# A graph network's attention layers: GpSimd gathers all source rows, with a pause for landing every 16, and TensorE's one-hot gathers go

## The chip, the cores and the metric

The kernel runs on one core of one Trainium2 chip. The metric is device time in microseconds of one execution; the kernel before takes 4386.61 us, the median of 3 runs (4384.65 to 4387.99).

## The reference

Four graph layers on 3125 nodes with 128 features and 100,000 edges, sorted by destination. Each is followed by a residual add and a layer norm. The first is a two-step GCN; the other three are attention layers (4, 8 and 4 heads), and the change is in these. Cut to what matters:

```python
x = (h @ W).reshape(n, H, C)                 # a row of 128 features per node
score = leaky_relu(a_src[src] + a_dst[dst])  # H numbers per edge
m = segment_max(score, dst);  p = exp(score - m[dst])
den = segment_sum(p, dst)
out = segment_sum(x[src] * (p / den[dst])[:, :, None], dst)
```

So every edge needs the row x[src] of its source node and that node's H source scores. The output has 3125 x 128 float32 values.

## The kernel before, in words

**Steps, blocks, groups.** 128 edges lie on the 128 partitions and make one step. A step never mixes two tiles of 128 destination nodes, so the 782 edge tiles become 806 real steps (REAL_STEPS). Eight steps are a block (U), 64 a group (GROUP); there are 101 blocks and 13 groups. The last group begins at step 760, so group 11 has 56 steps and group 12 has 46.

**A layer** is a `node_stage` (norms, the product with the weights, the table of rows written to HBM, per-node scores scattered to HBM by GpSimd, line 2016) and then `attend`. In `attend` a ring of 128 slots in SBUF (two groups) holds the gathered rows `m.ring`. For a group the order is:

- the rows arrive in the ring: GpSimd issues an indirect DMA per step, line 1400, each fetching 128 rows of 132 or 136 floats by the indices in `m.src`. It may reuse a slot when TensorE has finished the product of the step that held it (`product`);
- ScalarE copies the rows' score columns (line 1458), TensorE transposes them (line 1514), VectorE computes scores and running maxima (`score`, first line 1608), ScalarE takes exponentials;
- for each block: VectorE multiplies the rows by their coefficients (`message`, line 1685) and makes a one-hot of destinations (`onehot`, line 1691), TensorE multiplies the two (line 1554, two passes per step in the trace), VectorE adds the product to the node sums (`add_up`, line 1722), step by step at places that it loads into registers;
- VectorE prepares the destination scores of the next group (`spread`).

**TensorE's gathers.** Six of each group's 64 steps (AIDED) aren't gathered by DMA. The table is kept in SBUF as three bfloat16 parts that add up to float32 (`m.thirds`, made in `node_stage`, lines 1900, 1906, 1959, 1985). SyncE loads the six steps' source numbers broadcast to all partitions (line 1416). For 25 node tiles times two passes of three steps (50 units) ScalarE (lines 1439 and 1442) or VectorE (line 1387) makes a one-hot of sources, and TensorE multiplies it with the three parts (line 1497, three matmuls per unit) into three PSUM banks. VectorE adds the three parts and puts the rows into the ring (`take_aided`, lines 1701 to 1703). The units are laid by hand between the group's other work: CHAIN_HOTS, PART_HOTS and GAP_HOTS say how many go where, PART_DVE which of them VectorE makes. Group 0's units run at the start of the layer, those of group g+1 during group g.

**Queues.** GpSimd's queue in `attend` holds nothing but the waits for ring slots and the gathers. SyncE's queue holds, per group, the masks, the source numbers and the destination scores; the last wait in group 0 until the scatters of `node_stage` have landed (`m.scattered`), which is line 1424's first load.

Of the kernel before, what the change touches and what calls it, by code (L numbers as in the profile page):

```python
# [49 lines left out]
AIDED = 6  # L50
HOTS = 12
CHAIN_HOTS = (6, 2, 4)
PART_HOTS = (3, 3, 3, 4, 4, 4, 4, 4)
PART_DVE = (1, 1, 1, 1, 1, 1, 1, 1)
GAP_HOTS = (6, 3)
TAKEN_IN = (4,)
MIDDLE = NODE_TILES * P // 2
AHEAD_HOTS = sum(CHAIN_HOTS)
PASSES = AIDED // PER_BANK
UNITS = PASSES * NODE_TILES  # L60
WIDE_HOT = PER_BANK * P
# [17 lines left out]
assert AHEAD_HOTS + sum(PART_HOTS) + sum(GAP_HOTS) == UNITS and len(PART_HOTS) * U == GROUP and AIDED % PER_BANK == 0  # L79
assert CHAIN_HOTS[0] <= HOTS and AHEAD_HOTS <= HOTS and len(TAKEN_IN) == PASSES - 1  # L80
assert all(AHEAD_HOTS + sum(PART_HOTS[0:b]) == (n + 1) * NODE_TILES for n, b in enumerate(TAKEN_IN))
# [69 lines left out]
def allocate(nc, ctx, m):  # L151
# [20 lines left out]
    m.src_rows = m.arena[:, late:late + LANES // 2].bitcast(F16).rearrange("p (g e) -> p g e", e=P)  # L172
    assert late + LANES // 2 <= ARENA
# [27 lines left out]
    m.tile_low = sb("node_number_middle", [P, NODE_TILES])  # L201
    m.low_tile = sb("middle_node_number", [P, NODE_TILES])
# [19 lines left out]
    words = NODE_TILES * W // 2  # L222
    m.all_thirds = m.arena[:, at:at + 3 * words].bitcast(BF16).rearrange("p (t j f) -> p t j f", t=3, f=W)
    m.thirds = [m.all_thirds[:, i] for i in range(3)]
    at += 3 * words
    words = AIDED * P // 2
    m.aid_rows = [m.arena[:, at + h * words:at + (h + 1) * words].bitcast(F16) for h in range(2)]
    at += 2 * words
    words = WIDE_HOT // 2
    m.aid_far = [m.arena[:, at + h * words:at + (h + 1) * words].bitcast(F16) for h in range(2)]  # L230
    at += 2 * words
    m.aid_hot = [m.arena[:, at + h * words:at + (h + 1) * words].bitcast(BF16) for h in range(HOTS)]
    at += HOTS * words
# [20 lines left out]
    m.d_src_rows = dram("source_rows", [LANES, P], F16)  # L254
# [577 lines left out]
def load_counts_and_sum(nc, m, a):  # L832
# [28 lines left out]
    def mask(name):  # L861
# [3 lines left out]
         weights_in, rel_known, turned, rows_known, open_known, masks_known, stored) = phase(  # L865
        nc, "chunk_loaded_0", "chunk_loaded_1", "chunk_product", "unit_summed", "last_loaded", "dve_step", "begin_known", "begin_spread",
        "tiles_known", "j_turned", "j_out", "j_stored", "edges_gathered", "weights_gathered", "rel_known", "edges_turned",
        "source_rows_known", "open_known", "masks_known", "masks_stored")
# [4 lines left out]
    with ph, nc.Block(no_gpsimd_drain=True) as block:  # L873
# [15 lines left out]
        def _(sp):  # L889
# [14 lines left out]
            sp.wait_ge(rows_known, 1)  # L904
            sp.dma_start(m.d_src_rows.rearrange("(g p) e -> p g e", p=P), m.src_rows).then_inc(stored, 16)
# [3 lines left out]
            sp.wait_ge(stored, 48)  # L909
# [55 lines left out]
        def _(dve):  # L965
# [19 lines left out]
            def steps_known():  # L985
                chain(dve.tensor_tensor(j_of, step, t_of, ALU.subtract))
                chain(dve.tensor_copy(m.step_tile[:], t_of))
                chain(dve.tensor_scalar(m.step_base[:], j_of, float(P), None, ALU.mult))
                chain(dve.tensor_scalar(j_cap, j_of, float(NODE_TILES - 1), float(F + 8), ALU.min, ALU.mult))
                dve.engine_nop().then_inc(tiles_known, 1)  # L990
                chain(dve.memset(m.row_keep[:], 0.0))
                chain(dve.memset(m.row_back[:], NEG))
                chain(dve.tensor_scalar(m.tile_low[:], m.node_no[:], -float(MIDDLE), None, ALU.add))
                chain(dve.tensor_scalar(m.low_tile[:], m.tile_low[:], -1.0, None, ALU.mult))

            def edges_known():
# [5 lines left out]
                dve.tensor_scalar(m.src_rows, src, -float(MIDDLE), None, ALU.add).then_inc(rows_known, 1)  # L1002
# [288 lines left out]
def attend(nc, m, H, a, weighted, self_loops):  # L1291
# [12 lines left out]
    aid_banks = m.psum[:, 5 * 512:8 * 512].rearrange("p (k c) -> p k c", c=512)  # L1304
# [5 lines left out]
             "group_scored", "cleared", "aid_rows_in_0", "aid_rows_in_1", "far_known", "aid_hot_act", "aid_hot_dve", "hot_used", "aid_taken",  # L1310
             "table_back", "dve_step")
# [3 lines left out]
         group_scored, cleared, aid_rows_in0, aid_rows_in1, far_known, hot_act, hot_dve, hot_used, aid_taken, table_back, dve_step) = phase(nc, *names)  # L1315
    masks_in, spread_in = (masks_in0, masks_in1), (spread_in0, spread_in1)
    aid_rows_in = (aid_rows_in0, aid_rows_in1)
# [10 lines left out]
    def place(s):  # L1328
        g = sum(s >= lo_of(k) for k in range(1, GROUPS))
        return s - lo_of(g)  # L1330

# [17 lines left out]
    by_dve = set()  # L1349
    part_of = []  # L1350
    for n, own in zip(PART_HOTS, PART_DVE):
        lo = part_of[-1][-1] + 1 if part_of else AHEAD_HOTS
        part_of.append(range(lo, lo + n))
        by_dve.update(part_of[-1][n - own:])
    in_gap = range(UNITS - sum(GAP_HOTS), UNITS)

    def parts_of(g, b):
        blocks = blocks_of(g)
        return range(b - blocks[0], len(part_of) if b == blocks[-1] else b - blocks[0] + 1)

    def made_by_dve(g, u):
        return u % 2 == 1 if g == 0 else u in by_dve

    def made(g, u):
        return sum(made_by_dve(k, v) == made_by_dve(g, u) for k in range(g + 1) for v in range(UNITS if k < g else u + 1))

    def tails_of(g):
        return sum(1 + (lo_of(k) % SLOTS + size_of(k) > SLOTS) for k in range(g + 1))

    def hot_of(g, u):  # L1370
        return m.aid_hot[(g * UNITS + u) % HOTS]

    def rows_of(g, u):
        return m.aid_rows[g % 2][:, u // NODE_TILES * WIDE_HOT:(u // NODE_TILES + 1) * WIDE_HOT]

    def wait_for_hot(eng, g, u):
        n = g * UNITS + u
        if n >= HOTS:
            eng.wait_ge(hot_used, n - HOTS + 1)
        if u == 0 or g == 0 or u in by_dve:  # L1380
            eng.wait_ge(aid_rows_in[g % 2], 16 * (g // 2 + 1))

    def hot_on_dve(dve, g, u):
        wait_for_hot(dve, g, u)
        hi = u % NODE_TILES
        odd = lambda view: view.rearrange("p (a e) -> p a e", a=3)
        dve.tensor_scalar(odd(hot_of(g, u)), odd(rows_of(g, u)), m.tile_low[:, hi:hi + 1], None, ALU.is_equal).then_inc(hot_dve, 1)  # L1387
# [4 lines left out]
    with ph, nc.Block() as block:  # L1392

        @block.gpsimd
        def _(pool):
            for b in range(BLOCKS):
                if b * U >= SLOTS:
                    pool.wait_ge(product, min((b + 1) * U, REAL_STEPS) - SLOTS)
                for s in gathered(b):
# [4 lines left out]
        def _(sp):  # L1404
            for g in range(GROUPS):
# [26 lines left out]
        def _(act):  # L1432
            far = [0]

            def hot_on_act(g, u):
                wait_for_hot(act, g, u)
                hi = u % NODE_TILES
                away = m.aid_far[far[0] % 2]
                act.activation(away, rows_of(g, u), ACT.Abs, bias=m.low_tile[:, hi:hi + 1]).then_inc(far_known, 1)  # L1439
# [878 lines left out]
```

## Time and profile before

| | |
|---|---|
| three runs | 4384.65, 4386.61, 4387.99 us |
| the profiled execution | span 5825.1 us; no other time of it is on record |
| instructions in the trace | 61632 |
| busy: PE, DVE, ACT, POOL | 3173.4, 3165.7, 2409.4, 2312.0 us |
| mean granted TensorE clock | 0.753 |

The profiled execution's span is 1438.5 us longer than the median of the runs. Times in the rows are microseconds from the start of the span, unless marked ns. PE is TensorE's matmul, PEld its weight load, DVE is VectorE, ACT ScalarE, POOL GpSimd, SP SyncE; L1400 is line 1400 of the kernel. A row's last part, after the bar or in brackets, is idle time of the engine before the instruction and what ended it, as far as the profile can tell.

### The profile page before, as it was taken

To read this page: it belongs to the slowest core of one execution; us is meant where nothing else is said; L and a number is where in the kernel's file an instruction comes from. 1 tells how busy PE (TensorE), PEld (TensorE's weight loads), DVE (VectorE), ACT (ScalarE), POOL (GpSimd) and SP (SyncE) were. 2 spreads that over 40 slices of the span, in tenths; PEclk is the share of its full clock that TensorE was granted. 3 is DMA by queue.
4 is the path that set the end of the run, shared out by engine and by line. 5 is a ranking of instruction groups with operands and counts; after the bars stand their busy time and mean duration, and the time that the engine had idled before them with its cause. 6 is when DMAs were issued, how large, how long until landed. Compare 5 with 4: busy or idle time off the path is not lost. (4 is left out here: it accounts for less than half of the span.)

```text
span 5825.1 us, 61632 instructions
## 1 busy us (share of the span) xinstructions
PE 3173.4 (54%) x16208; PEld 1958.6 (34%) x16208; DVE 3165.7 (54%) x10115; ACT 2409.4 (41%) x5229; POOL 2312.0 (40%) x2409
## 2 busy tenths in 40 slices
PE   2888787623555555562155554555523555564563
PEld 1333343312333333342033333333311333343342
DVE  5999853513454554576064464555822455454466
ACT  0766630023444444443143443444433444444453
POOL 3000002074555455415545545544064545545422
PEclk7999998856777677786577777777756777777786
DMA  2111124221212222111112212211021212212110
GB/s 75 60 60 60 60 85 168 99 62 36 48 46 48 47 47 50 42 28 37 42 45 48 52 44 48 50 46 44 4 55 37 47 47 47 50 45 47 45 25 23
DMA packets 127624, 298.46 MB, mean 51 GB/s; under 512 B 45412, under 2 KB 74972, under 8 KB 123712
## 3 DMA queue, kind: packets, MB, share of 16 engines
q0 software_dynamic: 74976, 155.58, 11.6%
q1 hardware_dynamic: 52320, 139.24, 7.1%
q8 instruction: 116, 1.90, 0.1%
q14 instruction: 212, 1.74, 0.1%
HBM read 241.28 MB, written 53.38 MB: 51 GB/s over the span
## 5 line engine op out<-in xcount | busy, mean ns | idle before, releaser
L1400 POOL DMA_INDIRECT work<-table,lane_src x2184 | 2072.7, 949 | 1897.4 <-PE psum L1554 967.3
L1439 ACT ACTIVATE work<-work,middle_node_number 128x384 f16<-128x384 f16 x1587 | 958.0, 604 | 1997.8 <-DMA work<-table,lane_src 950.8
L1497 PE MATMUL psum<-work 128*128 128x396 bf16 (+1 forms) x5850 | 1360.1, 380 | 699.7 <-issue 464.9
L1554 PE MATMUL psum<-work 128*128 128x136 f32 x4836 | 827.7, 339 | 1004.9 <-DVE node_sums L1722 890.6
L1722 DVE TENSOR_TENSOR node_sums<-node_sums,psum 128x136 f32 x2418 | 561.3, 294 | 1455.8 <-remote 892.2
L1554 PEld LDWEIGHTS psum<-work 128*128 128x128 f32 x4836 | 778.8, 242 | 1085.0 <-issue 969.9
L1497 PEld LDWEIGHTS psum<-work 128*128 128x128 bf16 x5850 | 626.3, 109 | 1290.0 <-issue 758.1
L1442 ACT ACTIVATE work<-work 128x384 bf16<-128x384 f16 x1587 | 829.4, 523 | 50.4
L715 PE MATMUL psum<-work 128*128 128x448 f16 x2100 | 460.9, 358 | 47.4 <-issue 37.5
L744 DVE TENSOR_SCALAR work<-work 128x400 f16<-128x400 f16 x1568 | 468.3, 320 | 0.0
L772 PE MATMUL psum<-work 128*128 128x400 f16 x1568 | 342.1, 342 | 111.8 <-DVE work L744 90.9
L1685 DVE TENSOR_TENSOR work<-work,psum 128x1024 f32<-128x1024 f32 (+1 forms) x303 | 367.3, 1213 | 7.3 <-ACT work L1477 4.4
L1691 DVE TENSOR_TENSOR work<-psum,lane_dst_rel 128x1024 f32<-128x1024 f32 (+1 forms) x303 | 365.1, 1216 | 1.3
L880 POOL DMA_INDIRECT work<-in_dst,step_edge_tile x7 | 6.7, 951 | 829.3 <-DVEq L990 827.4
L743 DVE TENSOR_SCALAR work<-work 128x128 f16<-128x128 f16 x1176 | 295.0, 251 | 10.0 <-PE psum L772 5.9
L715 PEld LDWEIGHTS psum<-work 128*128 128x128 bf16 x2100 | 207.7, 99 | 232.8 <-issue 59.4
L810 ACT CAST work<-psum 128x400 f16<-128x400 f32 x392 | 192.9, 492 | 188.0 <-PE psum L772 184.1
L1701 DVE COPY work<-psum 128x396 f32<-128x396 f32 (+1 forms) x78 | 44.6, 571 | 368.9 <-DMA work<-table,lane_src 209.6
L709 DVE TENSOR_TENSOR node_sums<-node_sums,psum 128x16 f32 x784 | 132.5, 169 | 204.6 <-issue 183.4
L772 PEld LDWEIGHTS psum<-work 128*128 128x128 f16 x1568 | 127.0, 99 | 332.8 <-DVE work L744 193.1
L1387 DVE TENSOR_SCALAR work<-work,node_number_middle 128x384 bf16<-128x384 f16 x363 | 112.9, 319 | 223.6 <-DMA work<-table,lane_src 81.0
L2016 POOL DMA_INDIRECT spread<-node_spread,node_pos_first x75 | 72.8, 971 | 327.8 <-DVEq L1893 263.4
(360 smaller groups left out, 2539.9 us busy)
## 6 DMA issues: line engine op xcount, KB each, us to landing
counts<-work SPq DMA_DIRECT2D x14, 2800.0 KB, 8.1
work<-counts SPq DMA_DIRECT2D x14, 2800.0 KB
work<-table,lane_src POOLq DMA_INDIRECT x2184
work<-spread SPq DMA_DIRECT2D x78, 256.0 KB
work<-masks SPq DMA_DIRECT2D x78, 128.0 KB
work<-source_rows SPq DMA_DIRECT2D x39, 192.0 KB
spread<-node_sums SPq DMA_DIRECT2D x4, 896.0 KB
table<-work SPq DMA_DIRECT2D x10, 330.0 KB
```

Source lines behind the costliest of these rows:

```text
L715: t = pe.matmul(sum_bank(m, q), m.parts[part][:, hi, :], m.counts[q][:, :, hi * CW:(hi + 1) * CW], start=(hi == 0 and part == 0), stop=(hi ...
L743: dve.tensor_scalar(m.hot_lo[:, d, b, :], m.iota_cols[:, 0:P], m.low[:, b, bass.ds(n, 1)], None, ALU.is_equal)
L744: t = dve.tensor_scalar(m.hot_key[:, d, b, :], m.iota_cols[:], m.key[:, b, bass.ds(n, 1)], None, ALU.is_equal)
L772: t = pe.matmul(unit_bank(k), m.hot_lo[:, d, b, :], m.hot_key[:, d, b, :], start=(b == 0), stop=(b == CB - 1))
L1400: pool.indirect_dma_start(m.ring[:, s % SLOTS, 0:F + H], None, m.d_table[H], bass.IndirectOffsetOnAxis(ap=m.src[:, s:s + 1], axis=0)).then ...
L1439: act.activation(away, rows_of(g, u), ACT.Abs, bias=m.low_tile[:, hi:hi + 1]).then_inc(far_known, 1)
L1442: act.activation(hot_of(g, u), away, ACT.Relu, bias=1.0, scale=-1.0).then_inc(hot_act, 1)
L1497: mm = pe.matmul(aid_banks[:, k, 0:3 * (F + H)], hot_of(g, u)[:, k * P:(k + 1) * P], m.all_thirds[:, :, hi, 0:F + H], start=(hi == 0), sto ...
L1554: pe.matmul(sum_slot(s), m.onehot[b % 2][:, s % U, :], m.ring[:, s % SLOTS, :], start=True, stop=True).then_inc(product, 1)
L1685: dve.tensor_tensor(rows, rows, over(coef.unsqueeze(3), [P, n, H, C]), ALU.mult).then_inc(messages, 1)
L1691: dve.tensor_tensor(m.onehot[b % 2][:, 0:n, :], over(counted.unsqueeze(1), [P, n, P]), over(m.drel[:, b * U:b * U + n].unsqueeze(2), [P, n ...
L1722: dve.tensor_tensor(to, to, sum_slot(s), ALU.add).then_inc(summed, 1)
```

## The change

GpSimd gathers every step (`steps_of(b)` in place of `gathered(b)`). Before the gathers of each even block but the first it waits until those of the two blocks before have landed (`rows_in` at `landed(k)`). All of TensorE's gathers go: the one-hots on ScalarE and VectorE, the matmuls, the takes, the broadcast loads, the thirds of the table in `node_stage` and the source rows stored in the set-up. In `node_stage` the product of block b waits for the copies to the table (`tables`) where it waited for the thirds. The products of a block of steps use two alternating sets of three PSUM banks, where there was one set, so that a product waits for the sums of two blocks before.

```diff
-AIDED = 6
-HOTS = 12
-CHAIN_HOTS = (6, 2, 4)
-PART_HOTS = (3, 3, 3, 4, 4, 4, 4, 4)
...
-    def gathered(b):
-        return [s for s in steps_of(b) if place(s) >= AIDED]
-
     def landed(b):
-        return 16 * sum(len(gathered(k)) for k in range(b, -1, -(SLOTS // U)))
+        return 16 * sum(len(steps_of(k)) for k in range(b, -1, -(SLOTS // U)))
...
     def sum_slot(s):
-        at = (2 + s % U // PER_BANK) * 512 + s % U % PER_BANK * W
+        at = (2 + s // U % 2 * BLOCK_BANKS + s % U // PER_BANK) * 512 + s % U % PER_BANK * W
         return m.psum[:, at:at + W]
...
                 if b * U >= SLOTS:
                     pool.wait_ge(product, min((b + 1) * U, REAL_STEPS) - SLOTS)
-                for s in gathered(b):
+                if b % 2 == 0 and b:
+                    for k in (b - 2, b - 1):
+                        pool.wait_ge(rows_in[k % (SLOTS // U)], landed(k))
+                for s in steps_of(b):
                     pool.indirect_dma_start(m.ring[:, s % SLOTS, 0:F + H], None, m.d_table[H],
...
-                if g >= 2:
-                    sp.wait_ge(hot_used, (g - 1) * UNITS)
-                sp.dma_start(m.aid_rows[g % 2], m.d_src_rows[own.start:own.start + AIDED, :].rearrange("(a s) e -> a (s e)", a=1)
-                             .to_broadcast([P, AIDED * P])).then_inc(aid_rows_in[g % 2], 16)
...
-                    if b == blocks_of(g)[0]:
-                        act.wait_ge(aid_taken, (g + 1) * PASSES)
-                    if gathered(b):
-                        act.wait_ge(rows_in[b % (SLOTS // U)], landed(b))
+                    act.wait_ge(rows_in[b % (SLOTS // U)], landed(b))
...
-                if g + 1 < GROUPS:
-                    for u in range(AHEAD_HOTS, UNITS):
-                        if u not in by_dve:
-                            hot_on_act(g + 1, u)
...
-            aid(0, range(UNITS))
             turn_spread(0)
...
-                        if s % U % PER_BANK == 0 and s >= U:
-                            pe.wait_ge(summed, bank_end(s - U))
+                        if s % U % PER_BANK == 0 and s >= 2 * U:
+                            pe.wait_ge(summed, bank_end(s - 2 * U))
...
-                    for n in parts_of(g, b):
-                        aid(g + 1, part_of[n])
...
-            for u in range(UNITS):
-                if u % 2:
-                    hot_on_dve(dve, 0, u)
-                if u % NODE_TILES == NODE_TILES - 1:
-                    take_aided(0, u // NODE_TILES)
...
-                    if g + 1 < GROUPS and n in TAKEN_IN:
-                        take_aided(g + 1, TAKEN_IN.index(n))
...
-                    dve.tensor_tensor(product, product, high[:, j, :], ALU.subtract).then_inc(rest_known, 1)
...
-                    dve.tensor_tensor(low[:, j, :], out_part(b, n)[:, :, 0:F + H], middle[:, j, :], ALU.subtract).then_inc(thirds_known, 1)
...
                 if b >= 2:
-                    pe.wait_ge(thirds_known, len(parts) * (b - 1))
+                    pe.wait_ge(tables, per_block * (b - 1))
...
-                    act.copy(middle[:, j, :], out_part(b, n)[:, :, 0:F + H]).then_inc(middle_taken, 1)
...
-                    act.copy(high[:, c * BLK + lo:c * BLK + hi, :], out_part(c, n)[:, :, 0:F + H]).then_inc(high_taken, 1)
```

## Rows read from the trace of the kernel before

**Rows 1.** The page: span, and each engine's busy time and share.

```profile
span 5825.1 us, 61632 instructions
...
PE 3173.4 (54%) x16208; PEld 1958.6 (34%) x16208; DVE 3165.7 (54%) x10115; ACT 2409.4 (41%) x5229; POOL 2312.0 (40%) x2409
```

**Rows 2.** Line 1400: durations in ns (least/median/most); idle time before (us, times).

```profile
L1400 POOL DMA_INDIRECT work<-table,lane_src x2184: 938/944/1103, 1196.4 to 5595.4; - x199
...
  PE psum L1554: 967.3, 63
  issue: 617.1, 2025
```

**Rows 3.** Timeline of POOL, layer 2: start, duration, instruction, idle before.

```profile
3526.56 0.94 POOL L1400 DMA_INDIRECT work<-table,lane_src  x1 [0.30 <-issue]
3527.81 0.94 POOL L1400 DMA_INDIRECT work<-table,lane_src  x1 [0.30 <-issue]
3532.13 0.94 POOL L1400 DMA_INDIRECT work<-table,lane_src  x1 [3.38 <-DMA work<-source_rows]
```

**Rows 4.** Windows of the layers, line 1400: length, busy (count), clock, DMA share, GB/s.

```profile
1194.00:2627.00 1433.00, 695.05 (x728) 0.72 0.19 45
...
sum 4330.00, POOL 2072.70; mean POOL 690.90
```

**Rows 5.** Windows of groups: length; busy PE, PEld, DVE, ACT, POOL; PEclk; DMA; GB/s.

```profile
2336.00:2441.00 105.00, 59.79 (x302) 39.00 (x301) 54.15 (x145) 47.91 (x98) 49.59 (x52) 0.73 0.18 44
2530.00:2590.00 60.00, 47.53 (x282) 32.14 (x280) 49.26 (x135) 39.41 (x81) 0.00 (x0) 0.90 0.00 1
2590.00:2627.00 37.00, 19.94 (x108) 17.54 (x108) 30.66 (x89) 1.56 (x5) 0.00 (x0) 0.70 0.18 46
```

**Rows 6.** Timeline of all engines at the end of one stretch, layer 2.

```profile
3532.00 1.82 DVE L1722 TENSOR_TENSOR node_sums<-node_sums,psum 128x136 f32 x8 [12.48 <-DMA work<-source_rows]
...
3532.87 3.97 PE L1554 MATMUL psum<-work 128*128 128x136 f32 x16 [12.63 <-DVE node_sums L1722]
```

**Rows 7.** The waits of the whole span: engine, line, releaser; us, times, longest.

```profile
DVE node_sums L1722 <- remote: 892.2, 91, 14.8
...
DVE node_sums L1722 <- DMA work<-source_rows: 442.6, 47, 15.3
```

**Rows 8.** Timeline of the closing group of layer 1.

```profile
2587.40 0.83 ACT L1458 COPY work<-work 128x32 f32<-128x32 f32 x6 [6.05 <-DVE work L1703]
...
2610.11 1.80 DVE L1722 TENSOR_TENSOR node_sums<-node_sums,psum 128x136 f32 x8
...
2610.98 2.09 PE L1554 MATMUL psum<-work 128*128 128x136 f32 x16 [1.13 <-DVE node_sums L1722]
...
2614.10 1.80 DVE L1722 TENSOR_TENSOR node_sums<-node_sums,psum 128x136 f32 x8
```

**Rows 9.** Timelines of POOL and SP: each layer's last scatter, SP's next load.

```profile
1195.14 0.97 POOL L2016 DMA_INDIRECT spread<-node_spread,node_pos_first  x1 [0.31 <-issue]
...
1197.86 1.08 SPq L1424 DMA_DIRECT2D work<-spread  x2
...
2729.96 0.96 POOL L2016 DMA_INDIRECT spread<-node_spread,node_pos_first  x1 [0.30 <-issue]
...
2733.54 1.08 SPq L1424 DMA_DIRECT2D work<-spread  x2
...
4280.26 0.95 POOL L2016 DMA_INDIRECT spread<-node_spread,node_pos_first  x1 [0.30 <-issue]
...
4282.36 1.08 SPq L1424 DMA_DIRECT2D work<-spread  x2
```

**Rows 10.** The page, groups of instructions: two that go.

```profile
L1439 ACT ACTIVATE work<-work,middle_node_number 128x384 f16<-128x384 f16 x1587 | 958.0, 604 | 1997.8 <-DMA work<-table,lane_src 950.8
L1497 PE MATMUL psum<-work 128*128 128x396 bf16 (+1 forms) x5850 | 1360.1, 380 | 699.7 <-issue 464.9
```

**Rows 11.** Timeline of POOL, the third node stage's first scatter.

```profile
4244.52 1.09 POOL L2016 DMA_INDIRECT spread<-node_spread,node_pos_first  x1 [41.60 <-DVEq L1893]
```

More of the change, by code:

```diff
@@ L14 @@
-import itertools
 from contextlib import ExitStack
@@ L171, in allocate @@
     late += CCOLS // 2
-    m.src_rows = m.arena[:, late:late + LANES // 2].bitcast(F16).rearrange("p (g e) -> p g e", e=P)
-    assert late + LANES // 2 <= ARENA
+    assert late <= ARENA
     m.row_keep = sb("row_keep", [4, GROUPS, GROUP + 1])
@@ L221, in allocate @@
     at += 4 * P
[L222 to L233, printed above, removed]
     assert at <= ARENA
@@ L1477, in _ @@
                         act.copy(slots(lo_of(g) + lo, hi - lo)[:, :, F:W], coefs[:, lo:hi, :]).then_inc(tails, 1)
-                if g + 1 < GROUPS:
-                    for u in range(AHEAD_HOTS, UNITS):
-                        if u not in by_dve:
-                            hot_on_act(g + 1, u)
-                if g + 2 < GROUPS:
-                    for u in range(CHAIN_HOTS[0]):
-                        hot_on_act(g + 2, u)
         @block.tensor
         def _(pe):
-            def aid(g, units):
-                if g >= GROUPS:
-                    return
-                for u in units:
-                    n, hi = divmod(u, NODE_TILES)
-                    pe.wait_ge(hot_dve if made_by_dve(g, u) else hot_act, made(g, u))
-                    if hi == 0 and g * PASSES + n:
-                        pe.wait_ge(aid_taken, g * PASSES + n)
-                    for k in range(PER_BANK):
-                        mm = pe.matmul(aid_banks[:, k, 0:3 * (F + H)], hot_of(g, u)[:, k * P:(k + 1) * P], m.all_thirds[:, :, hi, 0:F + H],
-                                       start=(hi == 0), stop=(hi == NODE_TILES - 1))
-                    mm.then_inc(hot_used, 1)
             def turn_spread(g):
@@ L1515, in _ @@
                 t.then_inc(scores_turned, 1)
-                aid(g + 1, range(0, CHAIN_HOTS[0]))
                 pe.wait_ge(maxima_scanned, 2 * HL * (g + 1))
@@ L1692, in onehot @@
                                   over(m.drel[:, b * U:b * U + n].unsqueeze(2), [P, n, P]), ALU.is_equal).then_inc(hot, 1)
-            def take_aided(g, n):
-                third = [aid_banks[:, :, i * (F + H):(i + 1) * (F + H)] for i in range(3)]
-                lo = lo_of(g) + n * PER_BANK
-                rows = slots(lo, PER_BANK)[:, :, 0:F + H]
-                dve.wait_ge(hot_used, g * UNITS + (n + 1) * NODE_TILES)
-                if lo >= SLOTS:
-                    dve.wait_ge(product, lo + PER_BANK - SLOTS)
-                chain(dve.tensor_copy(rows, third[2]))
-                chain(dve.tensor_tensor(rows, rows, third[1], ALU.add))
-                dve.tensor_tensor(rows, rows, third[0], ALU.add).then_inc(aid_taken, 1)
-                dve.wait_ge(aid_taken, g * PASSES + n + 1)
             def places_of(lo, n):
@@ L1893, in scores @@
                 dve.engine_nop().then_inc(spread_known, 1)
-            def rest(b):
-                dve.wait_ge(high_taken, len(parts) * (b + 1))
-                for n, (lo, hi) in enumerate(parts):
-                    j = slice(b * BLK + lo, b * BLK + hi)
-                    product = out_part(b, n)[:, :, 0:F + H]
-                    dve.tensor_tensor(product, product, high[:, j, :], ALU.subtract).then_inc(rest_known, 1)
-            def lowest(b):
-                dve.wait_ge(middle_taken, len(parts) * (b + 1))
-                for n, (lo, hi) in enumerate(parts):
-                    j = slice(b * BLK + lo, b * BLK + hi)
-                    dve.tensor_tensor(low[:, j, :], out_part(b, n)[:, :, 0:F + H], middle[:, j, :], ALU.subtract).then_inc(thirds_known, 1)
-            for wave in range(TURNS + last + 3):
+            for wave in range(TURNS + last + 2):
                 for i, step in enumerate(steps):
@@ L1921, in _ @@
                 b = wave - last - 2
-                if 0 <= b < TURNS:
-                    if self_loops:
-                        scores(b)
-                    rest(b)
-                if b >= 1:
-                    lowest(b - 1)
-            dve.wait_ge(thirds_known, len(parts) * TURNS)
+                if self_loops and 0 <= b < TURNS:
+                    scores(b)
         @block.tensor
```

103 lines of the change are left out of this document (9 added, 94 removed).

## The prediction

> **What bounds the kernel now.** I read the totals first: no engine is busy over 54% of the span [rows 1], so busy time alone names no bound. The list of line 1400 has 2184 row gathers issued by GpSimd, 944 ns each by the median, and 617.1 us of "issue" gaps before 2025 of them, 0.305 each [rows 2]. That is 0.944 + 0.305 = 1.25 us per gather, and the timeline shows this very beat, whatever else is going on: 0.94 busy, 0.30 idle [rows 3].
>
> The next thing to see is that the profiled execution isn't the timed one. Its span is 5825.1 us, the only time of its own that is on record; the median of the three runs is 4386.6, 1438.5 us less. So before any sum I must know where the profile lost them. The windows by stage give the three attention layers 4330 us, the first 1433, with 728 gathers in each [rows 4]; everything else is 5825.1 - 4330 = 1495. One whole group of 64 steps takes 105 us while GpSimd gathers; a group of 56 steps after the last gather takes 60, and the last, of 46 steps, takes 37 to its end [rows 5]. In the first kind the timeline shows stretches in which VectorE starts its sums at 3532.00 after 12.48 us of idleness and TensorE its next products at 3532.87 after 12.63, while GpSimd went on with its beat until it, too, needed a semaphore that TensorE posts [rows 3, 6]. The sums (line 1722) wait for TensorE's products alone, but the list of waits puts theirs down to "remote" and to a load: 892.2 + 442.6 = 1335 us in 138 cases [rows 7]. That is near the 1438.5 us that the timed run doesn't have. I take them for something that profiling does and drop them.
>
> What is left can be summed in two ways. **GpSimd-bound:** a layer is 2.3 us to the first gather (1194 to 1196.4), 728 x 1.25 = 910, 2.7 until the last rows are in (below), and the closing group. That one runs from ScalarE's copy of its scores at 2587.40 to 2627, 40 [rows 5, 8]. Together 955, three layers 2865, with 1495 for the rest 4360: 27 under the median, 0.6%. **Chain-bound** (scores, messages, one-hots and sums passed between VectorE, TensorE and ScalarE): a block of 8 steps costs 4 us (sums at 2610.11 and 2614.10) [rows 8], so a full group is 60 + 4 = 64 and a layer 75 for the first 58 gathers, eleven groups of 64, one of 60 and the closing 40: 879; with the rest 4132, 255 under the median. The first fits. In the timed run the stream of gathers is the bound: 58 x 1.25 = 72.5 us per group against a chain of 64.
>
> **The change part by part.** *More gathers.* There are 806 real steps, 6 of each of 13 groups were not gathered, so 728 become 806: 78 x 3 x 1.25 = **+292.5 us**, all on the bounding engine.
>
> *The wait.* Blocks 2, 4, ... 100 first wait until the 16 gathers before them have landed: 50 times a layer, 150 in all. Queued behind it on GpSimd are only further gathers, which are what bounds. The trace has no wait for a gather's own landing. The nearest is SyncE, which waits for the last scatter GpSimd issued: scatter issued at 1195.14, 2729.96, 4280.26, the released load at 1197.86, 2733.54, 4282.36 [rows 9]. So 2.72, 3.58 and 2.10 us from issue to the waiting engine's going on. The next gather would have come 1.25 after; each wait costs 1.47 by the middle one, 0.85 to 2.33 by the ends. Whether a gather into SBUF is seen as late as a scatter to HBM, no row tells. The dearest row is GpSimd's own stop at 3527.81 with its next start at 3532.13 [rows 3]: 4.32, or 3.07 lost, but that one waits for TensorE. I take 1.47, since SyncE's rows wait for the same kind of thing: 150 x 1.47 = **+220.5 us**; the ends are 0 (the landing seen at once; time back is excluded, as nothing on GpSimd is seen to run faster after a pause) and 460. Another wait can't hide it: with GpSimd as the bound, its wait for ring slots is over long before.
>
> The Trainium skill, "DMA: Bandwidth & Descriptors", section "Anatomy of one DMA", fits one GpSimd-issued DMA at 2.0 us plus bytes over 436e3. For a gather of 128 x 132 x 4 bytes that is an estimate of 2.16 us, a wait of 0.91, and 136 us in place of 220: the time would be 4795. The trace's three cases lie at or above it (2.10, 2.72, 3.58).
>
> *What goes from the other engines.* ScalarE loses 1587 one-hots of two operations, the first 604 ns, TensorE 5850 matmuls of 380 ns [rows 10], VectorE its share of the one-hots and the sums of the thirds, SyncE a broadcast load per group and one store. None lies on the stream: worth 0 while the chain of 64 stays under the gathers, and without that cover the chain would only get shorter by them. The opening one-hots of group 0 are hidden behind its gathers too: 64 gathers and three waits, 84 us, come before its scores.
>
> *Node stages.* The splits into thirds go, four sets of ten operations per stage on VectorE and ScalarE. A stage ends with 25 scatters on GpSimd, the first at 4244.52 and the last at 4280.26 [rows 9, 11]: 35.7 us for 24 steps that need 24 x 1.25 = 30; at most 5.7 a stage is to be had, since some of the gaps are TensorE's and ScalarE's. **-10 us** for three, 0 to -17.
>
> **Sum.** 4386.6 + 292.5 + 220.5 - 10 = 4890. Built from the bottom instead: 2.3 + 806 x 1.25 + 50 x 1.47 + 2.7 + 40 = 1126 a layer, three 3378, + 1495 - 10 = 4863. The difference is the 27 of above; if they were waits for ring slots they vanish. I take **4880**. A full group is then 64 x 1.25 + 4 x 1.47 = 86 us against a chain of at most 64.
>
> **Rivals.**
> *Landing is cheap.* The beat already covers most of a transfer, and the wait costs 0.5 or less: 4386.6 + 292.5 + up to 75 - 10 = 4669 to 4744. For it: the timed run has no profiling traffic, and a gather is no scatter. Against: none of the three rows is under 2.10. 0.12.
> *The stop is dear, or TensorE slows.* If each wait costs the 3.07 of [rows 3], 4386.6 + 292.5 + 460 - 10 = 5129. Without the one-hot matmuls TensorE has less to do; its granted clock was 0.90 with them and no gathers, 0.70 in the closing group without [rows 5]. Sixteen passes of a block took 3.97 us once and 2.09 another time [rows 6, 8], about the ratio of the two levels (1.2 and 2.4 GHz), so at worst 8 x 1.9 = 15 us on a chain of 64: 79, still under 86. It decides only above 86, so the first half carries this case: 0.09.
> *Faster.* If profiling also slows the gathers, and TensorE's late semaphores are partly real, then before isn't bound by the stream but by those stalls, and both the pauses and the end of the one-hot matmuls relieve them. At a beat r the new layer is 806r + 50(2.72 - r) + 45; against the (4386.6 - 1495)/3 = 964 of now that wins only for r under 1.04. At r = 1.0: 806 + 86 + 45 = 937 a layer, and 3 x 937 + 1495 - 10 = 4296. For it: the profile's own 1438 us. Against: the beat doesn't move whether the others stand still or work, a gather lies between 938 and 1103 ns with 944 as the median [rows 2], and the GpSimd sum hits the median to 0.6%. 0.04.
> A rule that favours it: the Trainium skill, "SBUF — State Buffer", section "Who interferes with whom", has VectorE's 2-port modes lock GpSimd out of descriptor writing, and some of the removed one-hots may be such. By it gathers would quicken once they are gone; the trace shows next to none of that, with a median within 6 ns of the least, so it adds no gain.
> *Nothing measurable,* gains and losses cancelling near a beat of 1.04: 0.02.
>
> **Numbers.** Forecast 0.73, the others as given. The range covers the forecast's own ends (0.85 a wait gives 4797, 2.33 gives 5020), reaches half into the cheap case and leaves out the dear stop and the faster one: 4700 to 5010. A difference of 0.2% is about what a measurement of this kernel can tell from none. Faster 0.04, same 0.02, slower 0.94 (all the rest).
>
> **What the profile should show.** The gather line 2418 times at 0.94 to 0.95, beat 1.25, with 150 idle gaps of about 1.8 us (0.3 + 1.47) ended by the landing of rows. GpSimd's idle time before it for TensorE's products (967.3 us now [rows 2]) should fall. The stalls that only profiling brings may shrink, as the pauses come every 21.5 us, so the new span can lie nearer to its timed run than now. Wrong would be: gaps near 0.5 or over 3; a beat that isn't 1.25; or a chain over 86 us in groups where no engine stands still.

## The result and the profile after

The kernel after takes 4952.16 us (median of 4 runs, 4951.02 to 4954.76) against 4385.63 (4383.68 to 4387.99) for the one before on the same chip: 566.5 us more, a ratio of 1.129 [1.128, 1.131]. The forecast was 4880, the range 4700 to 5010. The profiled execution is itself one of the four, timed at 4951.02 with a span of 4949.3, so here nothing has to be dropped before the rows are summed.

On some chips the kernel before takes 4385 us in every run and on others 5815 to 5823 (medians), and its trace in [rows 1 to 11], with a span of 5825.1 and a clock of 0.753, agrees with the second kind (0.751 to 0.755), while the timed comparison ran on a chip of the first. I call the second kind disturbed; every ratio below is taken on one chip.

The page after, first of the whole, then the gathers (sections 1, 5 and 6), which answer to [rows 1, 2]:

```profile
span 4949.3 us, 45791 instructions
...
PE 1935.7 (39%) x10358; PEld 1364.9 (28%) x10358; DVE 2904.5 (59%) x9455; ACT 746.7 (15%) x1995; POOL 2553.8 (52%) x2643
...
L1320 POOL DMA_INDIRECT work<-table,lane_src x2418 | 2315.0, 957 | 1052.2 <-issue 693.4
...
work<-table,lane_src POOLq DMA_INDIRECT x2418, 2.5
```

GpSimd now issues 2418 gathers in place of 2184; ScalarE's busy time is down from 2409.4 to 746.7 and TensorE's from 3173.4 to 1935.7, and next to none of that shows in the time. The gather line by itself, with what ended GpSimd's idle time before it:

```profile
L1320 POOL DMA_INDIRECT work<-table,lane_src x2418: 938/946/1414, 1157.0 to 4798.5; - x186
its engine sat idle before it (us, times) until:
  issue: 693.4, 2260
  DMA work<-table,lane_src: 239.7, 101
  PE psum L1425: 119.0, 57
...
DMA to landing us min/median/max: 2.4/2.5/4.6
```

The last row is what no row of before could give: a gather lands 2.5 us after its issue. The two rows above it are the stops, 101 + 57 = 158 cases; 150 gaps of the trace are over 1.8 us long, 50 in each layer. That some are put down to TensorE says only which event the profile saw last: the kernel without the waits (below) has none over 1.8 us. One of them, in layer 2 (timeline of POOL: start, duration, instruction, idle before):

```profile
3113.90 0.94 POOL L1320 DMA_INDIRECT work<-table,lane_src  x1 [0.30 <-issue]
3115.15 0.94 POOL L1320 DMA_INDIRECT work<-table,lane_src  x1 [0.30 <-issue]
3118.54 0.94 POOL L1320 DMA_INDIRECT work<-table,lane_src  x1 [2.44 <-DMA work<-table,lane_src]
3119.79 0.94 POOL L1320 DMA_INDIRECT work<-table,lane_src  x1 [0.30 <-issue]
```

From issue to issue 3113.90 to 3115.15 is the beat, 1.25; 3115.15 to 3118.54 is 3.39. Over all 150 gaps of the trace the median is 3.3, so 2.05 lost by each. The windows of the three streams, from the first gather to the end of the last (those of [rows 4] are whole layers, with the closing group):

```profile
1156.90:2279.20 1122.30, 771.80 (x806) 0.61 0.25 58
2422.80:3551.40 1128.60, 775.70 (x806) 0.62 0.26 60
3683.80:4799.60 1115.80, 767.49 (x806) 0.62 0.25 58
sum 3366.70, POOL 2315.00; mean POOL 771.67
```

And who waits for that stream, from the list of waits:

```profile
ACT work L1356 <- DMA work<-table,lane_src: 2819.7, 267, 25.6
PE psum L1388 <- ACT work L1356: 1490.7, 39, 78.3
DVE work L1475 <- PE psum L1388: 1359.0, 39, 74.8
```

Unlike [rows 7], no wait of the sums for "remote" is there; that comes from the chip, since before on an undisturbed one has none either (below). The whole chain now hangs on rows landing: ScalarE's copy of the scores waits 2819.7 us for gathers, TensorE 1490.7 for that copy, VectorE 1359.0 for TensorE. A full group, from one score addition to the next, takes 88.5 to 90.5 us.

### The profile page after: what moved, and what is told of

The parts are those of the page before. It is cut to its first block and busy times, and to the rows that moved or that the text cites. A ratio compares the mean times of both kernels' runs of the same rounds, so it can differ in the third digit from the quotient of the medians.

```text
span 4949.3 us, 45791 instructions
## 1 busy us (share of the span) xinstructions
PE 1935.7 (39%) x10358; PEld 1364.9 (28%) x10358; DVE 2904.5 (59%) x9455; ACT 746.7 (15%) x1995; POOL 2553.8 (52%) x2643
## 3 DMA queue, kind: packets, MB, share of 16 engines
q14 instruction: 180, 1.47, 0.1%
## 5 line engine op out<-in xcount | busy, mean ns | idle before, releaser
L1320 POOL DMA_INDIRECT work<-table,lane_src x2418 | 2315.0, 957 | 1052.2 <-issue 693.4
L1425 PE MATMUL psum<-work 128*128 128x136 f32 x4836 | 808.6, 335 | 418.2 <-DVE node_sums L1577 319.9
L1425 PEld LDWEIGHTS psum<-work 128*128 128x128 f32 x4836 | 754.6, 238 | 478.0 <-issue 369.6
L1475 DVE TENSOR_TENSOR work<-psum,work 128x256 f32<-128x256 f32 (+1 forms) x39 | 20.0, 513 | 1359.0 <-PE psum L1388 1359.0
L1388 PE MATMUL psum<-identity,work 128*128 128x128 f32 x104 | 31.4, 431 | 1490.7 <-ACT work L1356 1490.7
L1356 ACT COPY work<-work 128x32 f32<-128x32 f32 (+2 forms) x303 | 79.7, 263 | 2819.7 <-DMA work<-table,lane_src 2819.7
L713 DVE TENSOR_SCALAR work<-work 128x400 f16<-128x400 f16 x1568 | 454.7, 309 | 0.0
L1388 PEld LDWEIGHTS psum<-identity,work 128*128 128x128 f32 x104 | 16.8, 210 | 1493.0 <-issue 1259.9
L684 PEld LDWEIGHTS psum<-work 128*128 128x128 bf16 x2100 | 207.7, 99 | 199.6 <-issue 26.4
L767 ACT ACTIVATE work<-work 128x128 f16<-128x128 f16 x394 | 159.0, 403 | 1.5 <-issue 1.0
L769 ACT ACTIVATE work<-work 128x128 f16<-128x128 f16 x394 | 121.9, 309 | 12.6
```

The source lines that it names most:

```text
L684: t = pe.matmul(sum_bank(m, q), m.parts[part][:, hi, :], m.counts[q][:, :, hi * CW:(hi + 1) * CW], start=(hi == 0 and part == 0), stop=(hi ...
L713: t = dve.tensor_scalar(m.hot_key[:, d, b, :], m.iota_cols[:], m.key[:, b, bass.ds(n, 1)], None, ALU.is_equal)
L767: act.activation(away, m.iota_cols[:, 0:P], ACT.Abs, bias=m.low_last[:, bass.ds(n, 1)], scale=-1.0).then_inc(lo_away, 1)
L1320: pool.indirect_dma_start(m.ring[:, s % SLOTS, 0:F + H], None, m.d_table[H], bass.IndirectOffsetOnAxis(ap=m.src[:, s:s + 1], axis=0)).then ...
L1425: pe.matmul(sum_slot(s), m.onehot[b % 2][:, s % U, :], m.ring[:, s % SLOTS, :], start=True, stop=True).then_inc(product, 1)
```

## The experiments

Each kernel is compared with before on its own chip. Some chips were disturbed (before at 5823.14 and 5815.6), the others not (4385.38, 4384.41, 4386.47). Each of these chips was seen in one session only, so what I call the chip could also be something of that session. The undisturbed ones come first, since the result is theirs.

**Increments once per bank.** In three kernels TensorE raises its product semaphore once per bank of up to three sums, not once per sum. The edit was made to see whether fewer increments mend the late ones of the disturbed chips (below). This chip was undisturbed, so it can't answer that; but the three kernels give before, after, and after without its waits under one condition, and a trace of before (with that edit) at its timed speed.

```diff
-                        pe.matmul(sum_slot(s), ..., start=True, stop=True).then_inc(product, 1)
+                        mm = pe.matmul(sum_slot(s), ..., start=True, stop=True)
+                        if s + 1 == bank_end(s):
+                            mm.then_inc(product, s % U % PER_BANK + 1)
```

and in the third kernel also

```diff
-                if b % 2 == 0 and b:
-                    for k in (b - 2, b - 1):
-                        pool.wait_ge(rows_in[k % (SLOTS // U)], landed(k))
```

> The kernel before, with TensorE posting its products once per PSUM bank (by 3, 3 and 2) in place of once per step: 3 increments a block in place of 8, same waits. Theory A (what stops VectorE and TensorE on these chips are TensorE's own increments, which come through one by one, some 3.5 us apart, while GpSimd gathers): where before takes 5820 this falls by several hundred us, at most to the 4386 that it takes elsewhere; the one-hot matmuls still post 50 a group, so 5000 to 5500. Rival (the late thing is TensorE's work itself, or it comes late in time whatever the count): within 1% of before. Where before takes 4386, no change: 4380 to 4390.

> The changed kernel with the same edit. Nothing else posts from TensorE in a block, so the increments fall from 8 to 3. Theory A: where before takes 5820, from 5523 down towards the 4952 of the undisturbed case, 5000 to 5150. Rival: 5450 to 5550. Where before takes 4386: 4952, as the stream of gathers and its stops bounds.

> The changed kernel without the waits for landing and with increments per bank. Where before takes 4386: 4637 (4952 less 150 stops of 2.1 us), which tests the price of the stops. Where before takes 5820: without stops 5720 was measured with 8 increments a block; theory A says 3/8 of the excess over 4637 is left, about 5050; the rival says 5700.

Measured: 4383.68, 4951.42 and 4649.54 us; ratios 0.9997 [0.9987, 1.0007], 1.1294 [1.1275, 1.1313] and 1.0602 [1.0584, 1.0619]. The edit changes nothing here, for before or for after. Without the waits 4637 was expected, 12 us less. The times split the change: 4649.5 - 4385.4 = 264 us for all but the waits, 4951.4 - 4649.5 = 302 for the waits.

The missing trace of before, as the kernel with increments per bank gives it, by its page, its gather line, its three streams (windows of line 1400) and its waits:

```profile
span 4380.9 us, 61632 instructions
...
PE 2856.4 (65%) x16208; PEld 1809.1 (41%) x16208; DVE 3163.1 (72%) x10115; ACT 2392.8 (55%) x5229; POOL 2338.4 (53%) x2409
```

```profile
L1400 POOL DMA_INDIRECT work<-table,lane_src x2184: 940/945/1427, 1161.5 to 4222.5; - x199
its engine sat idle before it (us, times) until:
  issue: 652.8, 2142
  PE psum L1554: 12.8, 42
```

```profile
1161.50:2082.80 921.30, 699.70 (x728) 0.84 0.29 68
2236.30:3166.20 929.90, 708.31 (x728) 0.84 0.30 70
3310.80:4223.50 912.70, 691.10 (x728) 0.84 0.30 68
sum 2763.90, POOL 2099.11; mean POOL 699.70
```

```profile
ACT work L1458 <- DMA work<-table,lane_src: 455.4, 73, 10.0
DVE work L1610 <- PE psum L1514: 440.1, 36, 31.3
```

Against [rows 2] the 967.3 us for TensorE are 12.8: GpSimd never stops from the first gather of a layer to the last. The first stream is 921 us long; in the trace of [rows 2, 4] it is 1315 (1196.4 to the end of the gather at 2511.35). This is the picture that the prediction reconstructed by leaving 1438.5 us out, with the beat that it took.

**Nine rows of a group by TensorE.** If the stream alone binds before, taking more gathers off it should pay as much as adding them costs.

```diff
-AIDED = 6
-PART_HOTS = (3, 3, 3, 4, 4, 4, 4, 4)
-PART_DVE = (1, 1, 1, 1, 1, 1, 1, 1)
-TAKEN_IN = (4,)
+AIDED = 9
+PART_HOTS = (4, 4, 5, 8, 8, 9, 8, 8)
+PART_DVE = (2, 2, 2, 4, 4, 5, 4, 4)
+TAKEN_IN = (3, 6)
```

(with the hots and takes of the extra part placed later in a block, and a take split where it crosses the end of the ring)

> The kernel before with nine rows of each group's 64 (or 56) gathered by TensorE in place of six, so 39 gathers fewer per layer and 117 in all; the hots, their places and the takes are spread over the group's blocks again, and three more of each part's hots are made. If the gather stream alone sets the time of before (a beat of 1.26 us, no stops), the run loses 117 x 1.26 = 147 us and takes some 4240 us where before takes 4385, and the gap to it is the mirror image of the change's 234 gathers (298 us). If the group's chain of scores, message work and sums (63 to 65 us without waiting for rows) or ScalarE, TensorE and VectorE with 50% more of TensorE's gathers on them bind instead, a group needs its 73 us or more still, and the run is at 4385 or above it, up to some 4500. On a chip where before takes 5820: the stream is no longer what binds there; if the late increments of TensorE hold the group, more of TensorE's gathers make it no faster, 5700 to 6000.

Measured: 4415.6 us, 1.0072 [1.0055, 1.0089]. The streams did shorten, by 132.6 us of the expected 147 (873.6 + 887.6 + 867.2 = 2628.4 in place of 2761.0, from first to last start), but a layer's last scores no longer follow its last gather. Timelines at the end of layer 1: GpSimd's last gather, then the copy of the last group's scores, in this kernel and, in the second fence, in before (the trace above):

```profile
2035.42 0.95 POOL L1400 DMA_INDIRECT work<-table,lane_src  x1 [0.30 <-issue]
...
2087.97 0.83 ACT L1458 COPY work<-work 128x32 f32<-128x32 f32 x6 [4.40 <-DVE work L1706]
```

```profile
2081.81 1.19 POOL L1400 DMA_INDIRECT work<-table,lane_src  x1 [0.30 <-issue]
...
2091.79 0.83 ACT L1458 COPY work<-work 128x32 f32<-128x32 f32 x6 [6.05 <-DVE work L1705]
```

10 us behind in before, 52.6 here: full groups now take 71.6, 75 and 72 us in the three layers, where 55 gathers need 69. The chain has become the bound. So the 10 us per group by which before's stream exceeds its chain are not to be had with nine rows; the rival of the expectation holds, and this kernel is no faster. A number between six and nine was not tried.

**Half the gathers, none of them waited for.** The other end: how short is the changed kernel's chain? The kernel leaves out every second gather from step 128 on, so its output is not the reference's; it is there for its time alone.

```diff
+    def fetched(b):
+        return [s for s in steps_of(b) if s < SLOTS or s % 2 == 0]
```

(used in place of `steps_of` for the gathers and in `landed`; no waits; increments once per bank)

> The kernel after without its waits, with TensorE's product semaphore raised once per bank, and with only the even steps gathered from step 128 on, so that the odd steps compute with rows that were gathered before (the output is not the reference's). GpSimd then issues some 32 gathers per group and can't be the bound. What is left is the chain of one group. If before was bound by GpSimd with the chain close behind, a group takes 63 to 65 us here and the run 3950 to 4070 us where before takes 4385. If something else in the group binds in all these kernels (the table's DMAs, VectorE's own work), a group still takes 72 us or more and the run is above 4300. On a chip where before takes 5820, this kernel with an increment for each step took 4454: if the number of TensorE's increments is what makes them late, it is well under that, near 4000; if the gathers in flight make them late, it stays at 4400 to 4500.

Measured: 3876.05 us, 0.8838 [0.8823, 0.8853], under both expectations. A full group takes 54, 58 and 54 us in the three layers, and here GpSimd waits for the chain:

```profile
L1320 POOL DMA_INDIRECT work<-table,lane_src x1401 | 1346.8, 961 | 764.8 <-issue 401.1 <-PE psum L1425 363.8
```

So the chain of the changed kernel needs at most 54 to 58 us of a group in which GpSimd needs 89. These are groups at a granted clock of 0.65 to 0.68, and after's streams ran at 0.61; but from a full group's score addition to its last sum both take the same, 44 to 46 us (48 to 50 in layer 2), so the lower clock doesn't change the answer. Before's chain is 63 to 66 (below): TensorE's gathers were worth some 9 us of it, all hidden.

**The waits alone, in before.**

```diff
+                if b % 2 == 0 and b:
+                    for k in (b - 2, b - 1):
+                        pool.wait_ge(rows_in[k % (SLOTS // U)], landed(k))
                 for s in gathered(b):
```

> The kernel before with the change's wait alone: TensorE still gathers six rows of each group, and at every second block GpSimd waits for the landing of the two blocks before. On a chip where before takes 4385 us. If a stop is a price of its own on the gather stream (2.03 us each, as between the changed kernel with and without its waits), the 150 stops add 300 and the run takes some 4690, a ratio of 1.07, and the two halves of the change add up: 264 for the gathers, 302 for the stops, 566 together. If the chain's slack or the room in the ring takes some of a stop here (the stream is only 10 us per group longer than the chain), it adds under 200, below 4590; if stops and TensorE's gathers get in each other's way, it adds over 400, above 4785. On a chip where before takes 5820 it is a repeat of the first run, 5930, a ratio of 1.02.

Measured: 4692.69 us, 1.0699 [1.0681, 1.0717]: 306.2 us more, 2.04 for each of 150 stops. It is the first theory's number. The gather line:

```profile
L1403 POOL DMA_INDIRECT work<-table,lane_src x2184: 938/947/1281, 1160.0 to 4531.4; - x199
its engine sat idle before it (us, times) until:
  issue: 611.4, 2006
  DMA work<-table,lane_src: 354.8, 140
```

By the time of the whole, the stops cost the same with TensorE's gathers beside them as without (306 and 302), and the parts of the change add up. The streams say a little more: they grew by 325 us (3086.4 for 2761.0), 2.17 a stop, and 19 us came back at the ends of the layers, where the last scores now start 5.6, 8.9 and 5.6 us after the last gather in place of 12.2, 14.4 and 12.9.

**The waits one block back, in after.**

```diff
-                    for k in (b - 2, b - 1):
+                    for k in [k for k in (b - 3, b - 2) if k >= 0]:
```

> The kernel after with each wait moved one block back: before block b GpSimd waits for blocks b-3 and b-2 and not for b-2 and b-1, so that the eight youngest gathers may still be on their way. On a chip where before takes 4385 us. If a stop costs because the queue is drained (the last gather must land, 2.5 us from its issue), there is no drain here, since a gather issued 10 us before has long landed, and the run takes what the kernel without waits takes, 4650, a ratio of 1.06. If the wait instructions themselves on GpSimd cost (300 of them, two for each stop), it takes most of the 302 us still, above 4850. On a chip where before takes 5820 it is a repeat of the first run, 5718, a ratio of 0.98.

Measured: 4649.83 us, 1.0602 [1.0585, 1.062], the same as without waits (4649.54). The same number of wait instructions, and next to no idle time for landing:

```profile
  issue: 713.8, 2342
  PE psum L1425: 19.8, 65
  DMA work<-table,lane_src: 3.4, 11
```

So the 302 us are not the price of waiting instructions but of an empty queue: GpSimd must see the last gather land before it may start the next.

**The disturbed chips.** What the kernel after and its variants do there.

> The kernel after without the waits for landing; all 64 gathers of a group stay. Theory 1 (the stream of gathers on GpSimd is the bound, and a wait costs what the profile of after shows, 3.3 us between two gathers in place of 1.25): 150 x 2.1 = 315 us less than after, so 4637, and 250 over before for the 234 more gathers. Theory 2 (the late semaphores of TensorE in before's profile are real in part, and the pauses relieve them): little is won, 4850 or more. Both expect the long stretches of idle VectorE to be back in the profile, with a span some 1000 us over the timed run; only theory 2 expects them in the timed run.

> The kernel before, with the waits for landing alone added (each second block, 150 of them, behind 14 or 16 gathers); TensorE's gathers stay. Theory 1: 150 x 2.05 = 308 us more than before, 4694. Theory 2: the pauses relieve TensorE, so less than half of that, or a gain. If before is held by the chain for part of the time, the waits hide there: 4550 to 4690. The profile's span should fall from 5825 to near the timed run in either.

> The kernel after with the same 150 waits, but each on the two blocks one further back, so that the eight newest gathers may still be in flight. Theory 1 (what costs is the stop until the newest gather has landed, 2.5 us from its issue): the older eight landed long before, the wait costs nothing, 4637 to 4650, like the kernel without waits. Rival: a wait on GpSimd costs by itself, whatever it waits for, since it holds the queue: up to 4950. Whether the profile keeps clean of the long stretches tells whether a pause or a bound on what is in flight removes them; I expect them back.

> The kernel after without the waits, and from step 128 on only every second step is gathered (the odd steps work on rows left in their slots from earlier). 403 + 64 gathers a layer can't be the bound, so this times the chain of VectorE, TensorE and ScalarE alone. From the rows: 1440 outside the layers, and a layer of 85 + 11 x 62 + 57 + 43 = 867: 4041. Theory 1 needs this to be well under before's 4386 and under 4637; a value over 4500 would say that the chain was near the bound all along.

> The changed kernel itself, beside before on the same chip as the runs so far or another one. In the first comparison before took 4386 and this one 4952; beside the four experiments before took 5823, with VectorE and TensorE standing still for stretches of 12 to 14 us while TensorE's increments of semaphores came late. Where before takes 4386 again, this takes 4952. Where before takes 5823: theory A (the stops for landing are too short to let the late increments through, since the long stretches end 3.4 us after the last gather's issue ends, and a stop here is over 2.1 us after it) says 5720 + about 150 to 315, so 5870 to 6035. Theory B (a stop each 16 gathers keeps the increments on time) says 4952.

The edits are the ones above (after_half_gathers with an increment for every sum; after_unchanged is the kernel after as it is). Measured, with the undisturbed time of the same kernel beside it where there is one:

| kernel | disturbed, us | ratio to before on its chip | undisturbed, us | difference |
|---|---|---|---|---|
| before | 5815.6 (and 5823.14) | 1 | 4385.4 | 1430 |
| before with the waits | 5932.06 | 1.0186 [1.0169, 1.0203] | 4692.7 | 1239 |
| after without waits | 5719.79 | 0.982 [0.9803, 0.9836] | 4649.5 | 1070 |
| after, waits one block back | 5718.02 | 0.9818 [0.9802, 0.9835] | 4649.8 | 1068 |
| after | 5523.31 | 0.9505 [0.9489, 0.9522] | 4952.2 | 571 |
| after, half the gathers | 4454.15 | 0.7646 [0.7634, 0.7659] | 3876.1 | 578 |

(The undisturbed time of the last row is of the kernel with an increment per bank, and that of the third too. After ran beside before at 5815.6, the other four beside 5823.14.) There the kernel after is 5% faster than before, where it is the slowest of all on the others.

Against what was expected: the forecasts by the stream alone (4694, 4637, 4637 to 4650, 4041) hold on undisturbed chips only. Before with the waits came out 109 us over before, under half of the stops' 308, as the second theory had it. For after neither theory was right, neither 5870 to 6035 nor 4952: with the waits it takes some 190 us less than without them.

 The stretches of [rows 6] are in every trace of these chips: the sums' waits for "remote" and for loads, 1335 us in [rows 7], are 1693 in after without waits and 1518 in after on such chips, and there are none in the undisturbed traces. After without waits, timeline of layer 1, with GpSimd's gathers left out:

```profile
2018.83 2.70 PE L1422 MATMUL psum<-work 128*128 128x136 f32 x16 [2.40 <-issue]
...
2034.20 1.82 DVE L1574 TENSOR_TENSOR node_sums<-node_sums,psum 128x136 f32 x8 [15.62 <-remote]
...
2038.54 3.96 PE L1422 MATMUL psum<-work 128*128 128x136 f32 x16 [17.01 <-DVE work L1555]
```

TensorE's 16 passes end at 2021.5 by the profile; VectorE, which waits for their semaphore alone, begins its sums at 2034.20. 12.7 us went by in which the profile shows nothing that the sums need at work, while GpSimd kept its beat. The increments of that semaphore stand in the trace at 2021.4, 2022.9, 2025.7, 2027.8, 2031.3 and 2034.1, right before VectorE goes on, then 2040.4, 2050.2 and 2051.6. GpSimd, which by then needs it too, issues nothing between 2047.2 and 2052.66, and twelve of them come together, 2052.3 to 2052.7. Two limits: the ends of matmuls are modelled, so the profile alone doesn't tell late increments from late work, though twelve in 0.5 us are closer together than products of 0.3 to 0.5 us each can end. And the trace has records of only 740 of this semaphore's 833 increments (of all 833 in after on an undisturbed chip), so no single record can be matched to its product. That VectorE, TensorE and GpSimd stand still waiting for each other's products is shown; that it is the increments that are late is the likelier reading.

What follows from the table: with the ring of slots full, these delays reach GpSimd too (102 gaps of over 1.8 us in after without waits, none on an undisturbed chip), so the stream alone is not the bound there. Full drains take 500 us off the difference in after (1070 to 571) and 190 off in before (1430 to 1239), at a price of 302 and 306; so the waits pay in after and not in before. The waits one block back, which drain nothing, take nothing off. Whether fewer increments would help there wasn't tried on such a chip, and why some chips do this, and how a drain relieves it, stays open.

## Why the prediction was right, and where it was off

**What bounds before: right for the timed runs.** The stream was put at 728 x 1.25 = 910 us a layer and measured 920, 929 and 912; the median gap is 1.25 and the mean 1.266. A chain of 64 for a full group was inferred; the group of 56 steps that ends a layer behind its stream takes 59.1, 61.8 and 59.4 between scores, so with 4 for a block 63 to 66. A full group takes 73.4, 74.1 and 72.6 in the three layers against the 72.5 worked out.

**The 1438.5 us: right to drop, wrong in the cause.** "I take them for something that profiling does" doesn't hold: a profiled execution of before with increments per bank has a span of 4380.9 on one chip, and timed runs of before have medians of 5815.6 and 5823.14 on others. The argument that the sum of GpSimd's beat hits the median carried the forecast; the guess about the cause did no work in it. But it hid a condition: on a disturbed chip the answer is 0.9505. That the comparison ran on one of the other kind no argument of the prediction secured; it was luck.

**More gathers: +292.5 worked out, 298.6 measured.** The three streams of after without waits sum to 3059.6 us against 2761.0 (first to last start), 234 gathers at 1.276. The beat is 1.25 by the median, and a tail of gaps between 1.3 and 1.6 us lifts its mean.

**The wait: the term that was mis-sized.** 1.47 each was taken, 220.5 in all; the streams of after sum to 3363.4, so 303.8 for 150, 2.03 each, and the times give 302. It lies within the ends given (0.85 to 2.33), nearer the dear one. The step that failed is the choice of SyncE's rows [rows 9] as the nearest. Their 2.72 from a scatter's issue to SyncE's going on is about what a gather's landing takes (2.5), but the engine that waited here is GpSimd, which started its next gather 3.3 after the last: 0.8 more than the landing (0.77 by the median of the 18 stops for which the trace has both). Its own stop in [rows 3] lost 3.07 and erred the other way. By the Trainium skill, "DMA: Bandwidth & Descriptors", section "Anatomy of one DMA", a gather of this size was estimated at 2.16 us; the trace has 2.5, and 4795 was further from the result than the sum that went by the rows.

**Node stages and the other engines: -10 worked out, -34 measured.** All that is outside the streams went from 1619.9 us (4380.9 - 2761.0) to 1585.9 (4949.3 - 3363.4). About 8 of it lies in the stages between the last scores of a layer and its successor's first gather or the end, and in the set-up; the rest, some 26, is a term that was missing: with its last group 40 gathers long, before's chain (59 to 62 us for the group before it) trails the stream at the end of each layer, while in after it doesn't. The scores of a layer's last group start 12.2, 14.4 and 12.9 us after its last gather in before, and 4.4, 4.8 and 4.3 in after. The latter, layer 1:

```profile
2278.16 0.95 POOL L1320 DMA_INDIRECT work<-table,lane_src  x1 [0.30 <-issue]
...
2282.60 0.42 DVE L1475 TENSOR_TENSOR work<-psum,work 128x256 f32<-128x256 f32 x1 [14.64 <-PE psum L1388]
```

The sum by measured terms: 4380.9 + 298.6 + 303.8 - 34.0 = 4949.3, the span. Against 4880: +83 for the stops, +6 for the gathers, -24 for the rest, +10 of rounding down from 4890, and -6 since the sum starts from a span of 4380.9 and not from 4386.6: 69 to the span, and 72 to the median of the runs.

**The rivals.** *Landing is cheap* fell with the first stop in the trace. *The stop is dear, or TensorE slows*: 2.03 isn't 3.07; the clock did fall, from 0.84 in before's streams to 0.61 in after's, and that cost nothing that shows, as the chain needs 54 to 58 of 89 us. *Faster*: its mechanism, TensorE's late semaphores being real and relieved by pauses and by the end of TensorE's gathers, fits what the disturbed chips show, 0.982 without the pauses and 0.9505 with them; its condition, a beat under 1.04, is not: the beat there is 1.25 as well. The rival should have been priced by the stalls and not by the beat. Of the expected marks, the gather count, the beat and the 150 gaps came out; the idle time of a gap is 2.3 us by the median (2.2 to 3.7), not 1.8; the median stays under the 3 that was to count as wrong.

## What to carry to other kernels

When one engine issues a stream that sets the time, a wait for the landing of its newest transfer empties the queue and costs the landing time plus that engine's own restart, less one beat (here 2.5 + 0.8 - 1.25); the same wait on transfers one block older bounds what is in flight and costs nothing. Before a gap between a profile and a timed run is blamed on the profiler, run the same kernel on another chip. And where two chains lie within 10 us of each other, as stream and chain of before, a large move of work pays in neither direction: 78 gathers a layer to GpSimd cost 264 us, 39 a layer to TensorE 31.

## What was not expected of the hardware

- Chips (or sessions, as each chip was seen once) differ by a third on the same kernel: before takes 4385 us on three or more and 5816 to 5823 on two, on each within 0.3% from run to run, and the change has the opposite sign (1.129 and 0.9505). What the traces of the second kind show is that VectorE's wait for TensorE's products ends late while GpSimd streams gathers: 12.7 us after the matmuls' end in the case shown.
- A gather of 128 rows of 528 or 544 bytes landed 2.5 us after issue by the median (2.4 to 4.6), and GpSimd, waiting for it, started its next 3.3 us after the last by the median, with TensorE's gathers beside it and without.
- TensorE at a granted clock of 0.61 in place of 0.84 cost the kernel nothing that shows: from a group's scores to its last sum after takes as long as the kernel with half the gathers at 0.65 to 0.68.
